# Gated cross-attention, experts, attention and FFN on one core: the middle stage's context, key weights and bias loaded and split inside the first attention's last units, and the opening's turns put first

## The chip, the cores and the metric

The kernel is one launch on one core of a Trainium2 chip. The metric is device time in microseconds, the median of three runs. All times below are microseconds unless they say ns.

## The reference

`x` is 2048 x 256, the context 1601 x 256, one batch. Four gated residual layers follow each other:

```python
x = x + tanh(g_xattn[0]) * L0_xattn(ctx, layernorm(x), mask, ...)  # 16 heads of 64; keys and values from the 1601 context rows and x
x = x + tanh(g_ffn[0]) * L0_ffn(layernorm(x), ...)                 # 8 experts, top 2, gelu
x = x + tanh(g_xattn[1]) * L1_xattn(layernorm(x), ctx, ...)        # 16 heads of 16, keys and values from the context
x = x + tanh(g_ffn[1]) * L1_ffn(layernorm(x), ...)                 # quantised, 1024 wide
```

The first attention runs over 3649 keys (2048 rows of `x` and 1601 of the context) for 2048 queries: in each layer softmax(q k^T) v, a product with the output weights, a gate, and the residual.

## The kernel before, in words

Four stages follow each other, each a block of five instruction streams that synchronise by semaphores, with a barrier between stages: `stage_latent` (L122, the first attention), `stage_middle` (L1544, the experts together with the key and value projections of the second attention), `stage_cross` (the second attention) and a quantised feed-forward stage. Every product that must be near fp32 is made of three fp16 passes: a value is split into a high part (ScalarE casts) and a low part (the difference, on GpSimd or VectorE).

**First attention.** The work is cut into 8 groups of two heads and 4 query blocks of 512, 32 units in all; a unit runs over 29 tiles of 128 keys. For a tile, TensorE makes the scores (`scores`, L914), ScalarE the exponential into a ring of six buffers `prob` (`weigh`, L480), TensorE the product with the values (`values`, L929). The row sums are built by adding the 29 `prob` tiles: VectorE adds five of them (`dve_tiles`, `add`, L630), GpSimd the other 24 (`pool_tiles`, L348), and `add_up` (L354) joins the two sums on GpSimd. A `prob` buffer is free again when its product and its addition are done. `sums` (L937) spreads the total over partitions by a product with ones, VectorE inverts it in four pieces (L636) and multiplies (L641), `outputs` (L948) applies the output weights in two halves, and `residual` (L649) adds each half to `x`. These steps of unit w are placed by tile numbers into unit w + 1; for unit 31 they stand at the end. Beside this, the running maximum of the unit after is made from pairs of score blocks (`pair`, L885 on TensorE, L598 on VectorE); the pairs run 33 ahead (`lead`), so they end in unit 30.

**Opening.** Before the first unit, `x` and the context are normalised on VectorE (L692 for `x`, L699 for the context), turned by TensorE (`turn_rows`, L826), scaled and cast on ScalarE (L501, L506), and the low part is made on GpSimd (`row_low`, L364). Three staging rows (`staged`) are used in turn, so the ScalarE row n waits until the low part of row n - 3 is made. The context rows are filled by VectorE (`fill_ctx`, L709), with masked values that GpSimd makes (L404). The 20 projections of group 0 (`open_jobs`; 8 key chunks, 4 query blocks, 8 value groups; L845, L853) use four PSUM banks in the order of `open_uses`: five stand before the first pair, the rest after every second pair (`job_after_pair`). In the main loop, the order on TensorE at the first tile is pair 33, then the scores of tile 0.

**Middle stage.** At its start, SyncE issues the loads of the context (1601 KB), the weights of the second attention (four groups of 384.5 KB through two staging buffers), the bias and the expert weights. ScalarE and GpSimd scale and split them (`w_high` L1708, `c_high` L1719, `e_high` L1727, `w_split` L1648, `c_split` L1655, `e_split` L1663). `x` is measured (L1825), normalised (L1838), turned (L1954) and split. TensorE projects keys of group 0, routes (`route`, L1965), projects the values of all groups, then the keys of groups 1 to 3 (`project`, L1987, L1994; ScalarE evacuates, L1742, L1738; VectorE makes the low key part, L1854). Finished key groups are laid into `k_op` by 12 small DMAs each; the keys of group 2 share a buffer with those of group 0, and of group 3 with group 1, so ScalarE's evacuation of group 2 waits until the 12 DMAs of group 0 have landed. The laying waits also for `ones_of` (L1668), which GpSimd does last of all. After that the 32 expert steps run (`first` L2010, `spread` L2020, `second_layer` L2036). The first `spread` waits for all projections and their low parts.

## Time and profile before

| | |
|---|---|
| median of three runs | 3250.26 (3250.1 to 3251.94) |
| the profiled execution: its own time | 3252.86 |
| its span, first to last instruction | 3251.1 |
| TensorE busy | 2952.4 (91%) |
| VectorE busy | 2419.8 (74%) |
| GpSimd busy | 2118.1 (65%) |
| ScalarE busy | 1806.9 (56%) |
| mean granted TensorE clock | 0.973 |
| DMA, mean over the span | 9 GB/s |

The span lies 1.8 below the execution's own time, which is launch and end around it. The page's 40 slices show TensorE at nine tenths or more everywhere but in the first slice and in the slices 29 and 30, where the first attention ends and the middle stage begins. The longest chain of waits on the page covers only the very end of the program, so the places of this change are read from the timeline and from busy times by stretch.

### The profile page before, as it was taken

The numbers are of one execution on the slowest core, as the hardware profiler recorded it, in microseconds if no ns is written. First come the engines' busy times: TensorE is split into PE (matmuls) and PEld (weight loads), VectorE is DVE, ScalarE is ACT, GpSimd is POOL, SyncE is SP. The second block draws the span as 40 slices with busy tenths as digits, with TensorE's granted clock in tenths as the row PEclk, the third lists the DMA queues.
The fourth block names the chain that finished last, engine by engine and source line by source line (L and its number), as shares of the span: only waits on it lengthen the run. The fifth ranks groups of instructions, "written<-read, shape, count | busy, mean of one in ns | idle before, by whom it ended". The sixth has DMA issues, their size and how long they took to land. (4 is left out here: it accounts for less than half of the span.)

```text
span 3251.1 us, 53579 instructions
## 1 busy us (share of the span) xinstructions
PE 2952.4 (91%) x21712; PEld 1091.0 (34%) x21720; DVE 2419.8 (74%) x2991; ACT 1806.9 (56%) x2025; POOL 2118.1 (65%) x1017
## 2 busy tenths in 40 slices
PE   5899999999999999999999999999498699999988
PEld 3233333333333333333333333322355123333235
DVE  8776787677777767777777876774435888888878
ACT  4455555455445555545555554545344388888875
POOL 5787988897898888889888888999520111111114
PEclk8999999999999999999999999999699699999999
DMA  1000000000000000000000000000210100000000
GB/s 62 6 1 1 1 8 1 1 7 1 1 7 1 1 1 7 1 1 7 1 1 1 3 1 1 1 1 1 68 33 9 46 7 7 8 7 7 7 1 27
DMA packets 24616, 28.73 MB, mean 9 GB/s; under 512 B 6511, under 2 KB 21296, under 8 KB 24370
## 3 DMA queue, kind: packets, MB, share of 16 engines
q1 hardware_dynamic: 24370, 25.31, 2.6%
q8 instruction: 172, 2.82, 0.4%
q14 instruction: 74, 0.61, 0.1%
HBM read 17.42 MB, written 2.10 MB: 6 GB/s over the span
## 5 line engine op out<-in xcount | busy, mean ns | idle before, releaser
L348 POOL TENSOR_TENSOR a_acc<-a_acc,a_prob 128x1024 f32<-128x1024 f32 x704 | 1725.3, 2451 | 299.5 <-ACT a_prob L480 217.7
L598 DVE TENSOR_REDUCE a_part_max<-wide 128x2 f32<-128x1024 f32 x880 | 1069.1, 1215 | 446.1 <-PE wide L885 445.3
L480 ACT ACTIVATE a_prob<-slot,a_mask_bias 128x1024 f32<-128x1024 f32 x928 | 986.9, 1112 | 740.7 <-PE slot L914 721.4
L929 PE MATMUL bank<-a_prob,a_val 128*64 128x512 f32 x3712 | 898.0, 606 | 2.1 <-ACT a_prob L480 2.1
L1218 ACT ACTIVATE a_prob<-slot,a_mask_bias 128x1024 f32<-128x1024 f32 x416 | 455.2, 1115 | 67.4 <-PE slot L1418 54.3
L885 PE MATMUL wide<-a_k_hi,a_q_hi 64*128 64x512 f16 (+1 forms) x2016 | 353.0, 362 | 113.8 <-DVE a_part_max L598 105.9
L1262 DVE TENSOR_REDUCE a_part_max<-wide 128x1 f32<-128x512 f32 x514 | 333.2, 682 | 37.7 <-PE wide L1406 21.0
L929 PEld LDWEIGHTS bank<-a_prob,a_val 128*64 128x64 f32 x3712 | 226.6, 136 | 394.2 <-issue 289.2
L914 PE MATMUL slot<-a_q_hi,a_k_lo 64*128 64x512 f16 x1856 | 352.7, 377 | 0.0
L914 PE MATMUL slot<-a_q_hi,a_k_step_hi 64*128 64x512 f16 x1728 | 328.2, 377 | 2.6 <-ACT a_prob L480 2.5
L914 PE MATMUL slot<-a_q_lo,a_k_step_hi 64*128 64x512 f16 x1728 | 328.0, 376 | 0.0
L885 PEld LDWEIGHTS wide<-a_k_hi,a_q_hi 64*128 64x128 f16 x2016 | 90.3, 93 | 551.4 <-DVE a_part_max L598 443.5
L1178 POOL TENSOR_TENSOR x_res<-a_gated,x_res 128x512 f32<-128x512 f32 x32 | 41.2, 1288 | 342.4 <-ACT a_gated L1230 342.2
L1432 PE MATMUL bank<-a_prob,a_val 128*32 128x256 f32 x3328 | 262.7, 392 | 0.1
L630 DVE TENSOR_TENSOR a_acc<-a_acc,a_prob 128x1024 f32<-128x1024 f32 x96 | 217.3, 2264 | 6.3 <-ACT a_prob L480 6.3
L1406 PE MATMUL wide<-a_k_op,a_q_op 48*128 48x512 f16 (+1 forms) x686 | 166.5, 355 | 36.6 <-DVE a_part_max L1262 29.0
L1262 DVE TENSOR_REDUCE a_part_max<-bank 128x1 f32<-128x512 f32 x254 | 173.3, 682 | 16.2 <-PE wide L1406 14.4
L1418 PE MATMUL slot<-a_q_op,a_k_op 64*128 64x512 f16 x832 | 160.9, 383 | 4.1 <-DMA a_q_op<-a_shift 2.8
L1166 POOL CAST a_hi<-a_y 128x512 f16<-128x512 f32 x15 | 9.2, 611 | 225.9 <-ACT a_y L1207 225.9
L636 DVE RECIPROCAL bank<-bank 128x128 f32<-128x128 f32 x128 | 120.7, 947 | 36.6 <-PE bank L937 36.6
L914 PEld LDWEIGHTS slot<-a_q_hi,a_k_lo 64*128 64x128 f16 x1856 | 90.5, 94 | 110.4 <-issue 0.8
L1406 PE MATMUL bank<-a_k_op,a_q_op 48*128 48x512 f16 (+1 forms) x338 | 109.6, 354 | 15.9 <-DVE a_part_max L1262 14.4
(398 smaller groups left out, 3275.0 us busy)
## 6 DMA issues: line engine op xcount, KB each, us to landing
a_w_staged<-in_w SPq DMA_DIRECT2D x8, 384.0 KB, 3.2
x_res<-in_x SPq DMA_DIRECT2D x4, 512.0 KB, 5.8
a_q_op<-a_hi SPq DMA_DIRECT2D x128, 16.0 KB, 1.8
out_x<-x_res SPq DMA_DIRECT2D x16, 128.0 KB, 1.7
a_k_op<-mid_k_hi SPq DMA_DIRECT2D x32, 52.0 KB, 2.2
mid_context<-in_ctxt SPq DMA_DIRECT2D x1, 1601.0 KB, 6.6
mid_w_staged<-in_w1a SPq DMA_DIRECT2D x4, 384.5 KB, 6.4
a_acc<-in_ctx SPq DMA_DIRECT2D x3, 512.0 KB, 8.4
```

Of the source, the lines that this page charges most:

```text
L348: nc.gpsimd.tensor_tensor(acc, before, prob[:, k % R, :], ALU.add).then_inc(added_p, 1)
L480: nc.scalar.activation(prob[:, k % R, :], m.slot[k % 2][:, :], ACT.Exp, bias=mbias[:, t:t + 1]).then_inc(probs_ready, 1)
L598: nc.vector.reduce_max(part_max[:, w % 2, :, j, c], pairs, AX.X).then_inc(max_used, 1)
L630: nc.vector.tensor_tensor(acc, before, prob[:, k % R, :], ALU.add).then_inc(added_v, 1)
L885: ins = nc.tensor.matmul(out, qh[g % 2][r, q0:q0 + P], src, start=True, stop=True, tile_position=(h * HALF, 0))
L914: ins = nc.tensor.matmul(score_bank(w, t, h), left, right, start=(whole and n == 0), stop=(n == len(terms) - 1), tile_position=(h * HALF, ...
L929: ins = nc.tensor.matmul(av[r, :], val[g % 2][:, t, r], prob[:, k % R, h * QB:(h + 1) * QB], start=(t == 0), stop=(t == NT - 1), tile_posi ...
L1218: nc.scalar.activation(prob[:, k % R, :], slot(("scores", w, s))[:, :], ACT.Exp, bias=mbias[:, t:t + 1]).then_inc(probs_ready, 1)
L1262: nc.vector.reduce_max(part_max[:, w % 2, 2 * z + h, j:j + 1, c], src, AX.X).then_inc(ring_used, 1)
L1406: ins = nc.tensor.matmul(bank(("max", n, h))[:, at:at + width_k], q_op[z][r, u * QB + j * P:u * QB + (j + 1) * P], k_op[g][z][r, k0:k0 + w ...
L1418: ins = nc.tensor.matmul(slot(("scores", w, s))[:, h * QB:(h + 1) * QB], k_op[g][z][r, t * P:(t + 1) * P], q_op[z][r, u * QB:(u + 1) * QB] ...
L1432: ins = nc.tensor.matmul(av[r, q], val[g][:, t, r], prob[:, (k + h // 2) % R, c0 + q.start:c0 + q.stop], start=(n == 0), stop=(n == a.halv ...
```

## The change

It does four things.

1. **Middle stage's inputs in the attention's last units.** A new function `keep_for_middle` lays one block of memory, `front_arena`, under the even buffers of the first attention (`k_hi`, `k_step_hi`, `q_hi`, `q_lo`, `val` of even groups). They are free after unit 27. From there the context, the weights of groups 0 and 1, the bias and the small expert arrays are loaded into them. GpSimd makes four memsets in unit 29; ScalarE scales and casts in unit 30 (`prepare`, 13 instructions behind odd tiles); VectorE makes the low parts and the bias in unit 31 (`prepare_low`). Three quarters of the statistics of `x` for the middle stage are taken in units 29 to 31 (`measure_final`). The second attention's `prob`, `y` and `bo` lie in the same block.
2. **Additions of the last unit.** In unit 31 VectorE adds nine tiles (`end_tiles`), GpSimd 20. `add_up` of unit 31 is gone: `sums` makes two accumulating products instead. The last inversion, multiplication and output product are done in halves, with a bank of their own for each half of the output.
3. **Middle stage.** It starts with key groups 0 and 1 (eight projections), two before each turn of `x`; then routing, the values of four groups, the keys of groups 2 and 3. `ones_of(0)` and `ones_of(1)` stand first on GpSimd.
4. **Opening.** Two projections stand before the first pair instead of five. GpSimd starts the low parts of `x` only after the normalisation of all `x`, and the masked values after the normalisation of the context. In unit 0, tile 0, the scores come ahead of pair 33.

```diff
+        self.job_after_pair = {1: keys_x[1], 3: keys_x[2], 5: keys_x[3], 7: keys_c[0], 9: v[0], 11: keys_c[1], 13: v[1], 14: queries[1],
+                               15: keys_c[2], 17: v[2], 18: v[3], 19: keys_c[3], 21: queries[2], 22: v[4], 23: v[5], 25: queries[3],
+                               27: v[6], 28: v[7]}
+        self.end_tiles = [3, 5, 7, 9, 13, 17, 21, 25, 27]
+        self.front_at = [(3, "scale", 0), (5, "keys", 0), (7, "queries", 0), (9, "scale", 1), (11, "keys", 1), (13, "queries", 1),
+                         (15, "router", 0)] + [(17 + 2 * c, "context", c) for c in range(4)]
+        self.low_at = [(1, "keys", 0), (2, "queries", 0), (3, "keys", 1), (4, "queries", 1), (5, "context", 0), (6, "context", 1),
+                       (7, "context", 2), (8, "context", 3), (13, "context", 4), (14, "context", 5), (15, "context", 6), (17, "context", 7),
+                       (19, "router", 0), (22, "bias", 0)]
...
+            sp.wait_ge(av_done, (last - NU + 1) * NT)
+            sp.dma_start(front.c32[:, :, 0:CTX], front.context.rearrange("(c p) t -> p c t", p=P)).then_inc(front_c, 16)
...
+            pool.wait_ge(normed, NL // 4)
+            row_low(0)
+            row_low(1)
             pool.wait_ge(w_first, 1)
             nc.gpsimd.tensor_tensor(w_lo[:, :], w_st[:, :], w_hi[:, :], ALU.subtract).then_inc(w_split, 1)
-            for n in range(6):
-                row_low(n)
+            row_low(2)
+            row_low(3)
+            pool.wait_ge(normed, len(cols))
             pool.wait_ge(mask_loaded, 32)
...
+            def divide_half(w, z):
+                dve.wait_ge(raw_ready, w + 1)
+                dve.wait_ge(inverted, a.pieces * w + a.pieces // 2 * (z + 1))
...
             def sums(w):
-                pe.wait_ge(total_ready, w + 1)
+                parts = [acc_p]
+                if w == last:
+                    pe.wait_ge(added_v, sum_v(w))
+                    pe.wait_ge(added_p, sum_p(w))
+                    parts = [acc_v, acc_p]
...
-        kinds = [("k", 0)] + [("v", g) for g in range(self.groups)] + [("k", g) for g in range(1, self.groups)]
+        kinds = [("k", 0), ("k", 1)] + [("v", g) for g in range(self.groups)] + [("k", 2), ("k", 3)]
...
-            turn(0, 0)
-            turn(0, 1)
-            project(0)
-            turn(0, 2)
-            project(1)
-            turn(0, 3)
-            project(2)
-            project(3)
+            for b in range(NB):
+                project(2 * b)
+                project(2 * b + 1)
+                turn(0, b)
             for b in range(NB):
                 route(b)
```

**Opening, GpSimd, before** (rows of the low parts, `xt_lo`, and of the masked values, `a_prob`; the names in brackets are the semaphores waited for):

```order
L398 TENSOR_TENSOR a_w_lo<-a_w_staged,a_w_hi 128x768 [waits a0_w_first,a0_wscale_set,a0_affine_loaded]
L362 COPY a_first_key<-a_k_full 128x1 [waits a0_rows_hi]
L363 TENSOR_TENSOR a_to_first<-a_affine_c,a_k_full 128x1
L364 TENSOR_TENSOR xt_lo<-a_k_full,xt_hi 128x512
L364 TENSOR_TENSOR xt_lo<-a_k_full,xt_hi 128x512 [waits a0_rows_hi] x4
L404 TENSOR_SCALAR a_prob<-a_valid_u,a_to_first,a_first_key 128x1664 [waits a0_affine_edge,a0_mask_loaded]
```

and of the change:

```order
L395 COPY a_first_key<-a_k_full 128x1 [waits a0_normed,a0_rows_hi,a0_wscale_set,a0_affine_loaded]
L396 TENSOR_TENSOR a_to_first<-a_affine_c,a_k_full 128x1
L397 TENSOR_TENSOR xt_lo<-a_k_full,xt_hi 128x512
L434 TENSOR_TENSOR a_w_lo<-a_w_staged,a_w_hi 128x768 [waits a0_w_first]
L397 TENSOR_TENSOR xt_lo<-a_k_full,xt_hi 128x512 [waits a0_rows_hi] x2
L441 TENSOR_SCALAR a_prob<-a_valid_u,a_to_first,a_first_key 128x1664 [waits a0_affine_edge,a0_mask_loaded,a0_normed]
```

Two low rows fewer stand before the masked values, and both places now wait for the normalised rows (`a0_normed`).

**Unit 31, VectorE, of the change** (`front_arena` holds the context and weights that came in; before, only four `a_acc` additions, four inversions, one multiplication and two residuals stood in this unit):

```order
L732 TENSOR_TENSOR front_arena<-front_arena 128x512
L735 TENSOR_TENSOR front_wq_lo<-front_arena,front_wq_hi 128x256
L751 TENSOR_TENSOR ct_lo<-front_arena,ct_hi 128x512 x2
L701 TENSOR_TENSOR a_acc<-a_prob 128x1024
L751 TENSOR_TENSOR ct_lo<-front_arena,ct_hi 128x512 x2
L701 TENSOR_TENSOR a_acc<-a_acc,a_prob 128x1024 x2
L707 RECIPROCAL bank<-bank 128x128 x2
L751 TENSOR_TENSOR ct_lo<-front_arena,ct_hi 128x512
L707 RECIPROCAL bank<-bank 128x128
```

In the whole unit twelve low parts of context and weights, the router's and three bias instructions are added, and VectorE has eight additions instead of four, beside GpSimd's 19 instead of 23.

**Start of the middle stage, TensorE, before** (`slot` from `ident` is a turn of `x`; `wide` and `bank` are key projections, `ct` the context):

```order
L1954 MATMUL slot<-ident,mid_xn 128x128 x16
L1987 MATMUL wide<-ct_hi,mid_kv_hi 128x512 x2
L1987 MATMUL wide<-ct_lo,mid_kv_hi 128x512 x2
L1987 MATMUL wide<-ct_hi,mid_kv_lo 128x512 x2
L1988 MATMUL wide<-mid_ones,mid_bias_op 128x512
L1954 MATMUL slot<-ident,mid_xn 128x128 x8
```

and of the change:

```order
L2093 MATMUL wide<-ct_hi,front_arena 128x512 x2
L2093 MATMUL wide<-ct_lo,front_arena 128x512 x2
L2094 MATMUL wide<-front_arena 128x512
L2063 MATMUL slot<-ident,mid_xn 128x128 x8
L2093 MATMUL bank<-ct_hi,front_arena 128x512 x2
L2093 MATMUL bank<-ct_lo,front_arena 128x512 x2
```

The projections lead; each turn of eight follows two of them.

## Rows read from the trace of the kernel before

**Rows 1.** Busy by stretch: time, five engines (PE, PEld, DVE, ACT, POOL), clock, DMA.

```profile
50.00:70.00 20.00, 16.12 (x145) 9.25 (x145) 19.59 (x21) 10.25 (x21) 14.75 (x16) 1.00 0.00 1
300.00:1000.00 700.00, 664.93 (x4392) 234.34 (x4392) 520.01 (x473) 364.19 (x410) 606.78 (x252) 1.00 0.01 3
2313.00:2336.00 23.00, 3.91 (x16) 3.14 (x16) 19.99 (x54) 9.26 (x18) 14.04 (x14) 0.50 0.65 221
```

**Rows 2.** Timeline of the opening, VectorE: start, length, what, idle before.

```profile
12.32 2.70 DVE L692 TENSOR_SCALAR a_prob<-x_res,a_mv,a_rstd 128x256 f32<-128x256 f32 x4
15.49 1.35 DVE L692 TENSOR_SCALAR a_prob<-x_res,a_mv,a_rstd 128x256 f32<-128x256 f32 x4
19.01 6.17 DVE L692 TENSOR_SCALAR a_prob<-x_res,a_mv,a_rstd 128x256 f32<-128x256 f32 x8
31.12 7.08 DVE L699 TENSOR_SCALAR a_acc<-a_acc,a_mv,a_rstd 128x256 f32<-128x256 f32 x13
46.10 0.75 DVE L709 SCALAR_TENSOR_TENSOR a_k_full<-slot,a_affine_c,a_prob 128x512 f32<-128x512 f32 x1 [7.30 <-PE slot L826]
49.69 1.22 DVE L598 TENSOR_REDUCE a_part_max<-wide 128x2 f32<-128x1024 f32 x1
91.26 1.22 DVE L598 TENSOR_REDUCE a_part_max<-wide 128x2 f32<-128x1024 f32 x1
```

**Rows 3.** Timeline of the opening, the other engines.

```profile
12.85 1.70 POOL L398 TENSOR_TENSOR a_w_lo<-a_w_staged,a_w_hi 128x768 f16<-128x768 f32 x1 [10.74 <-ACT a_w_staged L516]
28.57 1.15 POOL L364 TENSOR_TENSOR xt_lo<-a_k_full,xt_hi 128x512 f16<-128x512 f32 x1 [4.19 <-ACT xt_hi L506]
31.05 3.46 POOL L404 TENSOR_SCALAR a_prob<-a_valid_u,a_to_first,a_first_key 128x1664 f32<-128x1664 uint8 x2
92.62 0.61 PE L885 MATMUL wide<-a_k_hi,a_q_hi 64*128 64x512 f16 x2 [2.56 <-DVE a_part_max L598]
```

**Rows 4.** Unit 31's additions: group by line, and durations (ns min/median/max; VectorE's over all units).

```profile
L348 POOL TENSOR_TENSOR a_acc<-a_acc,a_prob 128x1024 f32<-128x1024 f32 x22 | 54.9, 2495 | 3.0
L348 POOL TENSOR_TENSOR a_acc<-a_acc,a_prob x22: 2337/2351/3155, 2240.1 to 2295.6; 128x1024 f32<-128x1024 f32 x22
L630 DVE TENSOR_TENSOR a_acc<-a_acc,a_prob x96: 1217/2172/3017, 121.4 to 2261.5; 128x1024 f32<-128x1024 f32 x96
```

**Rows 5.** Timeline of the attention's end.

```profile
2300.48 1.97 PE L937 MATMUL bank<-a_acc,a_ones 128*64 128x512 f32 x4 [15.07 <-POOL a_acc L354]
2302.50 3.40 DVE L636 RECIPROCAL bank<-bank 128x128 f32<-128x128 f32 x4 [36.59 <-PE bank L937]
2309.67 2.08 PE L948 MATMUL bank<-a_wo,a_att 128*128 128x256 f32 x4 [0.84 <-DVE x_res L649]
2311.79 0.75 DVE L649 SCALAR_TENSOR_TENSOR x_res<-bank,tanh_gates,x_res 128x512 f32<-128x512 f32 x1 [2.17 <-PE bank L948]
```

**Rows 6.** Middle stage, timeline; the DMA row is from its waits (total, times, longest).

```profile
2313.75 1.41 DVE L1825 BATCH_NORM_STATS2 mid_stats<-x_res 128x6 f32<-128x256 f32 x4
2317.35 2.48 DVE L1838 TENSOR_SCALAR mid_xn<-x_res,mid_mv,mid_rstd 128x256 f32<-128x256 f32 x4
2336.21 1.01 PE L1987 MATMUL wide<-ct_hi,mid_kv_hi 128*128 128x512 f16 x2 [5.99 <-DVE mid_bias_op L1869]
2340.69 1.29 DVE L1846 TENSOR_TENSOR xt_lo<-slot,xt_hi 128x512 f16<-128x512 f32 x2 [1.38 <-ACT xt_hi L1704]
2341.97 0.69 DVE L1854 SCALAR_TENSOR_TENSOR mid_k_lo<-wide,mid_k_hi 128x512 f16<-128x512 f32 x1
2347.18 0.29 DVE L1881 SCALAR_TENSOR_TENSOR mid_logits<-slot,moe_rb 128x128 f32<-128x128 f32 x1
2371.58 0.59 PE L2010 MATMUL slot<-xt_hi,mid_w_hi 128*128 128x512 f16 x2
ACT mid_k_hi L1742 <- DMA a_k_op<-mid_k_lo: 10.3, 2, 6.8
2394.58 0.58 PE L2020 MATMUL slot<-mid_wt_hi,mid_pick 128*128 128x512 f16 x1 [4.91 <-DVE mid_k_lo L1854]
```

More of the change, by code:

```diff
@@ L651, in measure, with measure_final @@
+            def measure_final(b):
+                dve.wait_ge(res_added, 2 * (last - NU + 1 + b) + 2)
+                for t in range(4 * b, 4 * b + 4):
+                    nc.vector.bn_stats(front.stats[:, t, :], m.x[:, t, :]).then_inc(front_measured, 1)
+                for t in range(4 * b, 4 * b + 4):
+                    dve.wait_ge(front_measured, t + 1)
+                    nc.vector.bn_aggr(front.mv[:, t, :], front.stats[:, t, :])
             def measure(src, t0, n):
@@ L980, in _ @@
                     n = w * NT + t + a.lead
+                    if w == 0 and t == 0:
+                        scores(w, t)
+                        pair(n)
+                        continue
                     if t % 2 == 0:
@@ L1003, in _ @@
                         project(*a.job_at[w * NT + t])
-            last = a.units - 1
             values(last, NT - 2)
@@ L1788, in _ @@
                 weights_high(g)
-                evacuate(NC + a.routing + g)
-            for p in range(NC + a.routing + NB, a.nj):
+                evacuate(a.front + a.routing + g)
+            for p in range(a.front + a.routing + NB, a.nj):
                 evacuate(p)
@@ L1906, in _ @@
                                         ALU.subtract).then_inc(wt_ready, 1)
-            for p in k_jobs[NC:]:
+            for p in k_jobs[a.front:]:
                 k_low(p)
@@ L2059, in _ @@
                 ins.then_inc(wt_turned, 1)
-                project(NC + a.routing + g)
+                project(a.front + a.routing + g)
             first(0)
             first(1)
-            for p in range(NC + a.routing + NB, a.nj):
+            for p in range(a.front + a.routing + NB, a.nj):
                 project(p)
```

499 lines of the change are left out of this document (281 added, 218 removed).

## The prediction

> **What bounds the kernel now.** I read the busy times by stretch first [rows 1]. In the attention's middle TensorE is busy 664.93 of 700 at clock 1.00: nothing is to be won there, and the change leaves it alone. At the start of the middle stage it is busy 3.91 of 23.00. Then the timelines of these places and of the opening, for who waits for whom.
>
> The opening: VectorE sits idle 7.30 before the first filled row, then makes 33 pairs nearly without a gap; the third starts at 49.69, the last at 91.26 [rows 2]. TensorE waits 2.56 for it, and only then makes pair 33 and the first scores [rows 3]. So VectorE sets the opening.
>
> Unit 31: GpSimd's 22 remaining additions take 54.9, with 3.0 of gaps, back to back: 2.495 each where the shortest takes 2.337 [rows 4]. TensorE gets the total at 2300.48, 15.07 late [rows 5]. GpSimd sets this unit.
>
> Middle stage: the first projection waits for the bias until 2336.21, routing is ready at 2347.18, the first expert matmul runs at 2371.58, the steps start at 2394.58, after ScalarE waited 10.3 for laying DMAs [rows 6].
>
> **Opening, part by part.** VectorE normalises four tiles in 1.35 alone and in 2.70 while a GpSimd operation of 1.70 runs beside it; eight take 6.17 beside the low rows [rows 2, 3]. GpSimd now keeps out: twelve tiles in 3 x 1.35 = 4.05 instead of 8.87, gain 4.8. The context's 13 tiles took 7.08; at 1.35 / 4 each they take 4.4, gain 2.7. They end at 38.2 - 7.5 = 30.7. One low part of a query (0.7), and the two first pairs run to 33.9, with the keys and queries that TensorE projected meanwhile. Here comes the new wait: GpSimd's masked values (3.46) start at 30.7 only, then low rows 4, 5 and 6 at 1.15 each [rows 3], 37.6, with row 7 of ScalarE and TensorE's turn of the context behind row 4. The fills (about 0.7 each) end at 38.7, where the third pair starts. It stood at 49.69: 11.0 earlier. From there VectorE's list is the old one, 91.26 + 1.22 - 49.69 = 42.8. Projections stand closer now (three behind consecutive pairs, twice), for which I charge 0.5. The first scores ahead of pair 33 fill part of TensorE's wait of 2.56 [rows 3]; between 0 and 2.56 I take 0.8. **Opening: -11.3.** Bounds: -6, if ScalarE's rows behind GpSimd cost 5 more; -14, if the removed gaps all count.
>
> **Units 28 to 31.** The loads go out on an idle SyncE queue, and the first who waits for them is GpSimd in unit 29, a whole unit later. ScalarE's 13 instructions in unit 30 stand behind odd tiles, where it waits for scores while TensorE makes the products: nothing. If this cover were gone, 13 x 0.69, the price of a 512-wide instruction [rows 6]: 9. The statistics (1.41 and 0.4 of aggregation [rows 6]) stand in VectorE's pair sequence in units 29 and 30, and TensorE's pairs wait for it: between nothing and 3.6 I take +1.0.
>
> In unit 31 GpSimd has 18 additions left instead of 22 and no joining. An undisturbed one is 2.337 plus its gap, 3.0 / 22 = 0.137: 2.474. VectorE's four additions and the rest lengthened them by 54.9 - 22 x 2.337 = 3.5, 0.87 for one. Now there are eight: 7.0. The low parts of context and weights, half as wide or less, I price at half: four before GpSimd reaches its second addition and six after, 2.1 + 1.9, the bias 0.5. GpSimd's 22 began at 2240.1; the 18 end at 2240.1 + 2.1 + 18 x 2.474 + 7.0 + 1.9 + 0.5 = 2296.1, against 2300.48: -4.4. `sums` doubles, +1.97 [rows 5]. The tail, 2302.50 to 2312.54 [rows 5], was four inversions (3.40), a multiplication, product, residual, product, residual: 10.0. In halves, with two banks: 3.40, two half multiplications at 0.4 (half a residual's 0.75), then one product (2.08) and one residual (0.75): 7.1, that is -2.9. **Unit 31 and tail: -5.3.** Bounds: 0, if every addition of GpSimd took nearly its longest, 3.155; -12, if VectorE disturbed nothing more than before.
>
> What the trace shows of the two engines is only that a VectorE addition of 1.217 at its shortest stretches to a median of 2.172, and GpSimd's to 3.155 [rows 4]. The Trainium skill, SBUF — State Buffer, "Who interferes with whom", says that a VectorE instruction with two SBUF inputs and a GpSimd one that reads SBUF exclude each other for a whole instruction. By it each new addition takes a full turn from GpSimd, and this is the second rival below.
>
> **Middle stage.** It starts as it did. Statistics of four tiles (1.41 and 0.4) instead of sixteen, the table load and square root to 2317.1, two normalisations beside GpSimd's memsets (2.48 and some 2.2 [rows 6]) and their waits: 2322.2. Then four blocks on VectorE: key low parts 6 x 0.6 + 2 x 0.25, turned low parts 4 x 1.25, two normalisations of 1.4 [rows 6] (a row's length overlaps the next by 0.1): 11.9, and 1.2 for waits on turns: 2335.3. TensorE's eight projections (two groups, 9.8), four turns (4) and a start at half clock (3) fit beside. With the last routing matmuls 2335.9, against 2347.0: -11.1. ScalarE then works down the same list as before, so the first expert matmul moves from 2371.58 to 2360.8. From there to the steps it was 23.0. A pair of 512-wide matmuls follows the next by some 0.43 (0.59 in the row of 2371.58 overlaps it), so a key chunk is 3 x 0.43 + 0.22 = 1.5 and a group, three chunks and a quarter, 4.9. Now two key groups remain instead of three, with 2.6 (six pairs) for the first expert matmuls and 1.2 for the last low part; the 10.3 for DMAs are gone, as group 0 and 1 are laid 25 earlier: 13.6, so -9.4. Sum -20.2; for the new rows' waits I take **-19.5**. Bounds: -13, if the waits between turns and low parts double and ScalarE's list starts 6 later; -22.
>
> **Sum.** -11.3 + 1.0 - 5.3 - 19.5 = -35.1. The profiled execution took 3252.86, 2.6 above the median; it would take 3217.8 with a span of 3216.0. On the median: 3250.26 - 35.1 = **3215.2**.
>
> **The rivals.**
> - *Opening held by GpSimd.* ScalarE's row 7, the turns and fills form a chain behind the masked values; if it costs 5 to 8 more, opening -3 to -6: about 3222. For it: three staging rows only. Against: it ends at 38.7, where before nothing of the pairs had begun.
> - *Strict turns on the shared memory path in unit 31.* Each of eight VectorE additions then takes 1.22 from GpSimd instead of 0.87, each low part 0.6 instead of 0.43: 2.8 + 1.8 = 4.6 more, 3219.8. For it: VectorE's median of 2.172. Against: four additions cost 3.5, not 4.9.
> - *All parts at their best bound*, GpSimd undisturbed: -14, -12, -22: 3203.
> - *The middle stage still waits*: its first projections cover little, because ScalarE's splitting list sets the first expert matmul. Then only the DMA wait and one key group go, -15: 3220.
> - *Slower: TensorE stays at 1.2 GHz.* Its work is now cut into short pieces between waits, in the opening from pair 2 on and in the middle stage's front. TensorE has 16.12 / 20 x 43 = 35 of work in the opening's last 43 [rows 1] and some 49 before the steps (eight groups of 4.9, 2.6, turns and routing 7). At half clock that is 70 and 98: the opening ends 16 after 92.5, the steps start 17 after 2394.58; with -5.3 and +1.0, 3279. It decides if the granted clock lies near 0.5 there. For it: clock 0.50 where TensorE had 3.91 of work in 23 [rows 1]. Against: 1.00 at 16.12 of 20 [rows 1], with the same pieces.
> - *The change has no effect*: a first projection that waits for its inputs again. The order has no such wait.
>
> **How the numbers follow.** Forecast 0.58, opening held 0.12, strict turns 0.09, all at best 0.08, middle waits 0.09, slower 0.03, no effect 0.01. A range from 3204 to 3229 takes in the forecast, three of the others whole and combinations of two of them. A measurement of this kernel can tell 0.2%, 6.5, from no change; only the clock rival lies above it. Faster 0.96, same 0.01, slower 0.03.
>
> **What would show it.** Third pair near 38.7; TensorE's pair 33 near 81.3, behind the first scores; a fill waiting for low rows near 37. In unit 31 (all 11 earlier) GpSimd's last addition 2.4 long some 56 after the joining of unit 30, then `sums` of 3.9. In the middle stage a projection at once, routing some 22 and steps some 61 after its start, no ScalarE wait for a DMA. I am wrong where the steps start over 67 after it, or where unit 31's additions average over 2.9.

## The result, and the profile after

| | before | changed |
|---|---|---|
| median of 4 runs, us | 3250.43 (3250.1 to 3251.94) | 3216.20 (3214.07 to 3217.43) |
| profiled execution, its span | 3251.1 | 3215.3 |

The ratio is 0.9893, 95% interval 0.9878 to 0.9909: 34.2 faster, where 35.1 were forecast. The profiled executions, cut at marks that both traces have (a unit's maxima complete, the shift of unit 31, the middle stage's first instruction, VectorE's first product of its steps):

| from ... to | before | changed | difference | forecast |
|---|---|---|---|---|
| start ... maxima of unit 1 | 151.38 | 139.69 | -11.7 | -11.3 |
| ... shift of unit 31 | 2070.44 | 2072.23 | +1.8 | +1.0 |
| ... start of the middle stage | 91.93 | 85.88 | -6.1 | -5.3 |
| ... VectorE's first product of the steps | 81.95 | 65.20 | -16.8 | -19.5 |
| ... end | 855.4 | 852.3 | -3.1 | 0 |

The pieces sum to 35.8, which is the difference of the two spans.

The timelines of the changed kernel (start, length, what, idle before). First the opening, VectorE's rows, which answer to [rows 2]:

```profile
12.28 1.38 DVE L802 TENSOR_SCALAR a_prob<-x_res,front_mv,a_rstd 128x256 f32<-128x256 f32 x4
...
17.04 2.67 DVE L802 TENSOR_SCALAR a_prob<-x_res,front_mv,a_rstd 128x256 f32<-128x256 f32 x8
26.65 4.29 DVE L809 TENSOR_SCALAR a_acc<-a_acc,front_mv,a_rstd 128x256 f32<-128x256 f32 x13
31.62 1.22 DVE L668 TENSOR_REDUCE a_part_max<-wide 128x2 f32<-128x1024 f32 x1
36.87 0.75 DVE L819 SCALAR_TENSOR_TENSOR a_k_full<-bank,a_affine_c,a_prob 128x512 f32<-128x512 f32 x1 [2.90 <-POOL xt_lo L397]
38.65 1.22 DVE L668 TENSOR_REDUCE a_part_max<-wide 128x2 f32<-128x1024 f32 x1
```

The forecast marks up to the third pair stand: normalisations of some 1.35 for four, their end near 31, a fill that waits for low rows at 36.87, the third pair at 38.65. TensorE makes the first scores before pair 33, which comes 1.8 later than forecast (81.3):

```profile
83.06 0.61 PE L1004 MATMUL wide<-front_arena 64*128 64x512 f16 x2 [0.28 <-DVE a_part_max L668]
```

This was 92.62 with a wait of 2.56 [rows 3]. Unit 31 and the attention's end, for [rows 4, 5], GpSimd, VectorE and TensorE:

```profile
2228.69 3.34 POOL L387 TENSOR_TENSOR a_acc<-a_acc 128x1024 f32<-128x1024 f32 x1
2231.99 23.47 POOL L381 TENSOR_TENSOR a_acc<-a_acc,a_prob 128x1024 f32<-128x1024 f32 x8
2255.89 29.65 POOL L381 TENSOR_TENSOR a_acc<-a_acc,a_prob 128x1024 f32<-128x1024 f32 x10 [0.43 <-POOL a_acc L381]
...
2229.73 5.61 DVE L751 TENSOR_TENSOR ct_lo<-front_arena,ct_hi 128x512 f16<-128x512 f32 x2
2264.61 2.73 DVE L743 CAST front_arena<-front_arena 2x1024 f16<-2x1024 f32 x1
2267.37 3.26 DVE L745 SCALAR_TENSOR_TENSOR front_arena<-front_arena,ident 2x1024 f16<-2x1024 f16 x1
...
2285.63 3.42 PE L1063 MATMUL bank<-a_acc,a_ones 128*64 128x512 f32 x8 [7.85 <-issue]
2289.10 1.78 DVE L707 RECIPROCAL bank<-bank 128x128 f32<-128x128 f32 x2 [10.72 <-PE bank L1063]
2295.78 0.75 DVE L726 SCALAR_TENSOR_TENSOR x_res<-slot,tanh_gates,x_res 128x512 f32<-128x512 f32 x1 [1.51 <-PE slot L1078]
```

GpSimd has 18 additions after the joining instead of 22, in 53.55. The tail, from the first inversion to the end of the last residual, takes 7.43 where it took 10.0. The middle stage, VectorE, for [rows 6]:

```profile
2297.80 1.40 DVE L1939 BATCH_NORM_STATS2 front_stats<-x_res 128x6 f32<-128x256 f32 x4
2301.49 7.35 DVE L1957 TENSOR_SCALAR mid_xn<-x_res,front_mv,mid_rstd 128x256 f32<-128x256 f32 x8
2311.16 1.36 DVE L1957 TENSOR_SCALAR mid_xn<-x_res,front_mv,mid_rstd 128x256 f32<-128x256 f32 x4
2323.09 0.29 DVE L1990 SCALAR_TENSOR_TENSOR mid_logits<-slot,front_rb 128x128 f32<-128x128 f32 x1 [0.93 <-PE slot L2072]
```

and GpSimd, TensorE and ScalarE there:

```profile
2297.73 5.90 POOL L1810 MEMSET a_k_op<- 128x1664 f16 x4 [12.20 <-POOLq L56]
2303.58 1.94 POOL L1814 MEMSET mid_wt_hi<- 128x2048 f16 x1
2305.47 1.94 POOL L1815 MEMSET mid_wt_lo<- 128x2048 f16 x1
...
2297.77 1.01 PE L2093 MATMUL wide<-ct_hi,front_arena 128*128 128x512 f16 x2 [2.03 <-PEq L56]
2307.61 1.97 PE L2063 MATMUL slot<-ident,mid_xn 128*128 128x128 f32 x8 [4.42 <-DVE mid_xn L1957]
...
2352.26 0.60 ACT L1869 ACTIVATE mid_k_hi<-wide 128x512 f16<-128x512 f32 x1 [3.69 <-PE wide L2094]
2360.99 1.28 ACT L1910 ACT_TABLE_LOAD   x1
```

TensorE projects at once, and no row of ScalarE waits for a DMA. But the eight normalisations take 7.35 instead of 4.7: the first four of them run beside GpSimd's memsets, each starts within one and ends about with it (0.72, 1.65, 1.97 and 1.96 long), and the other four, behind the last memset, have 0.4 each, as the next four have, 1.36 together. Routing is ready 25.3 after the start (forecast 22; before 33.4), the steps begin at 65.2 (forecast 61). The first expert matmul runs 50.16 after the start, before 57.83; from there to the steps it is 15.0 where it was 24.1.

### The profile page after: what moved, and what is told of

Read it like the earlier page. It is cut to its first block and busy times, and to the rows that moved or that the text cites. A ratio compares the mean times of both kernels' runs of the same rounds, so it can differ in the third digit from the quotient of the medians.

```text
span 3215.3 us, 53534 instructions
## 1 busy us (share of the span) xinstructions
PE 2952.3 (92%) x21716; PEld 1091.1 (34%) x21724; DVE 2459.1 (76%) x3006; ACT 1807.6 (56%) x2022; POOL 2099.6 (65%) x999
## 5 line engine op out<-in xcount | busy, mean ns | idle before, releaser
L527 ACT ACTIVATE a_prob<-slot,a_mask_bias 128x1024 f32<-128x1024 f32 x928 | 987.3, 1113 | 735.6 <-PE slot L1033 726.6
L1348 ACT ACTIVATE front_arena<-slot,a_mask_bias 128x1024 f32<-128x1024 f32 x416 | 455.3, 1116 | 63.0 <-PE slot L1548 49.6
L1048 PE MATMUL bank<-a_prob,a_val 128*64 128x512 f32 x1856 | 449.9, 607 | 0.2 <-ACT a_prob L527 0.2
L1048 PE MATMUL bank<-a_prob,front_arena 128*64 128x512 f32 x1856 | 447.6, 604 | 0.0
L1033 PE MATMUL slot<-front_arena 64*128 64x512 f16 x1856 | 276.7, 377 | 0.1
L1562 PE MATMUL bank<-front_arena,a_val 128*32 128x256 f32 x3328 | 261.5, 390 | 0.1
L1004 PE MATMUL wide<-a_k_hi,a_q_hi 64*128 64x512 f16 (+1 forms) x1024 | 179.4, 362 | 56.8 <-DVE a_part_max L668 53.1
L1004 PE MATMUL wide<-front_arena 64*128 64x512 f16 (+1 forms) x992 | 173.7, 363 | 57.1 <-DVE a_part_max L668 52.6
L1033 PE MATMUL slot<-a_q_hi,a_k_lo 64*128 64x512 f16 x928 | 176.8, 378 | 0.0
L1033 PE MATMUL slot<-front_arena,a_k_lo 64*128 64x512 f16 x928 | 176.3, 377 | 0.0
```

Of the source, the lines that this page charges most:

```text
L527: nc.scalar.activation(prob[:, k % R, :], m.slot[k % 2][:, :], ACT.Exp, bias=mbias[:, t:t + 1]).then_inc(probs_ready, 1)
L1004: ins = nc.tensor.matmul(out, qh[g % 2][r, q0:q0 + P], src, start=True, stop=True, tile_position=(h * HALF, 0))
L1033: ins = nc.tensor.matmul(score_bank(w, t, h), left, right, start=(whole and n == 0), stop=(n == len(terms) - 1), tile_position=(h * HALF, ...
L1048: ins = nc.tensor.matmul(av[r, :], val[g % 2][:, t, r], prob[:, k % R, h * QB:(h + 1) * QB], start=(t == 0), stop=(t == NT - 1), tile_posi ...
L1348: nc.scalar.activation(prob[:, k % R, :], slot(("scores", w, s))[:, :], ACT.Exp, bias=mbias[:, t:t + 1]).then_inc(probs_ready, 1)
L1562: ins = nc.tensor.matmul(av[r, q], val[g][:, t, r], prob[:, (k + h // 2) % R, c0 + q.start:c0 + q.stop], start=(n == 0), stop=(n == a.halv ...
```

## The experiments

All are edits of the changed kernel. The table has each one's time, the time of the kernel before beside it, and marks from its trace ("inversion": first inversion after the attention, from the shift of unit 31; "logits" and "table", ScalarE's table load ahead of the steps: from the middle stage's start). Each kernel has one trace.

| kernel | time / before | unit 1's maxima | inversion | logits | table |
|---|---|---|---|---|---|
| before | | 151.38 | 80.68 | 33.43 | 79.73 |
| changed | 3216.20 / 3250.43 | 139.69 | 77.18 | 25.29 | 63.19 |
| u31_five | 3223.03 / 3251.19 | 138.84 | 83.62 | 25.30 | 63.21 |
| u31_thirteen | 3215.36 / 3251.19 | 139.88 | 75.70 | 24.25 | 62.16 |
| u31_no_context_low | 3214.90 / 3251.19 | 138.63 | 75.35 | 24.44 | 62.34 |
| u31_bias_last | 3212.91 / 3251.70 | 141.73 | 72.69 | 25.49 | 63.38 |
| open_no_waits | 3217.31 / 3251.14 | 142.25 | 76.80 | 25.24 | 63.14 |
| open_old_order | 3227.17 / 3251.70 | 151.75 | 77.24 | 25.32 | 63.22 |
| open_pair_first | 3216.94 / 3253.42 | 141.87 | 77.33 | 25.46 | 63.36 |
| mid_memsets_behind | 3217.24 / 3251.19 | 139.13 | 77.35 | 25.30 | 64.83 |
| mid_memsets_last | 3212.16 / 3251.14 | 138.81 | 76.71 | 18.95 | 56.86 |
| mid_list_first | 3209.03 / 3251.14 | 139.72 | 76.65 | 19.33 | 55.99 |
| mid_one_key_group | 3223.19 / 3251.14 | 139.16 | 76.95 | 25.44 | 69.95 |
| all_together | 3205.90 / 3251.70 | 138.76 | 73.04 | 19.33 | 55.76 |

Where an edit leaves its piece alone, the inversion lies within 76.65 to 77.35 (8 kernels), the logits within 24.25 to 25.49, unit 1's maxima within 138.6 to 139.9 but for u31_bias_last, where the granted clock was lower there (told under open_pair_first). Whole runs differ by more than that for reasons told at the end, so the marks carry the verdicts.

### Unit 31: what does an addition on VectorE cost?

**u31_five.**

```diff
-        self.end_tiles = [3, 5, 7, 9, 13, 17, 21, 25, 27]
+        self.end_tiles = [5, 7, 9, 15, 17]
```

> The changed kernel with unit 31's additions divided as in every other unit: VectorE makes 4 of them instead of 8, GpSimd 22 instead of 18 after the joining of unit 30. In the changed kernel those 18 took 53.5 from 2231.99, 9.0 over 18 x 2.474. Theory A (the prediction's price: a VectorE addition costs GpSimd 0.87): GpSimd ends 4 x (2.474 - 0.87) = 6.4 later, time 3216.2 + 6.4 = 3222.6. Theory B (strict turns, 1.22 each): +5.0, 3221.2. Theory C (the 9.0 come from VectorE's low parts, its additions cost nothing): +9.9, 3226.1. GpSimd's mean addition in unit 31: 2.9 by A and B, 2.88 by C.

GpSimd's 22 additions, by line, from the joining on (total and mean in ns, then the gaps before them):

```profile
L381 POOL TENSOR_TENSOR a_acc<-a_acc,a_prob 128x1024 f32<-128x1024 f32 x22 | 57.2, 2599 | 3.3 <-POOL a_acc L381 0.4
```

The inversion comes 6.44 later (6.3 to 7.0 against the eight), so an addition moved is worth 1.61, and it costs GpSimd 2.474 - 1.61 = 0.86 (0.73 to 0.91): theory A. Strict turns (5.0) and free additions (9.9) fall. (The means in the expectation were worked out wrongly; by A it is (53.5 + 6.4) / 22 = 2.72, and the trace gives 2.60 with 0.15 of gap, 2.75.)

**u31_thirteen**: `end_tiles` with every odd tile from 3 to 27, thirteen of them, so VectorE makes twelve additions.

> The other direction: 13 tiles of unit 31 on VectorE, that is 12 additions, GpSimd has 14 after the joining of unit 30. A: GpSimd's last addition ends 6.4 earlier, 3209.8. B: 5.0 earlier, 3211.2. C: 9.9 earlier, of which 6.6 can count, since TensorE's last product of values ends at 2277.8 only, 7.8 before the sums. Theory D: VectorE, which has low parts, statistics and four quarters of inversion besides, is the later of the two now, its late additions keep ring places and ScalarE's exponentials wait for them: sums no earlier, 3216 to 3221.

Only 1.5 come. GpSimd's rows show why:

```profile
2232.38 24.26 POOL L381 TENSOR_TENSOR a_acc<-a_acc,a_prob 128x1024 f32<-128x1024 f32 x8
2262.14 2.36 POOL L381 TENSOR_TENSOR a_acc<-a_acc,a_prob 128x1024 f32<-128x1024 f32 x1 [5.50 <-ACT a_prob L527]
2266.88 2.36 POOL L381 TENSOR_TENSOR a_acc<-a_acc,a_prob 128x1024 f32<-128x1024 f32 x1 [2.37 <-ACT a_prob L527]
```

It is idle 9.85 for exponentials (five waits). VectorE's additions are late behind its low parts and the bias, the ring's places stay taken, and ScalarE waits. That is D's mechanism; the time it forecast (no gain) was a little too high. The next experiment moves the bias to try it.

**u31_bias_last**: thirteen tiles, and

```diff
-                       (19, "router", 0), (22, "bias", 0)]
+                       (19, "router", 0)]
...
                     add(last, t - 2)
+            prepare_low("bias", 0)
             for z in range(2):
```

> As the kernel with 13 tiles of unit 31 on VectorE, and its three instructions on the bias (6.7 beside GpSimd's additions) stand behind VectorE's last addition, where it waits for the sums. With 13 tiles alone the first inversion came 75.70 after the shift of unit 31 (77.18 in the changed kernel, 83.62 with 5 tiles), and GpSimd waited 9.9 for exponentials, which waited for ring places held by VectorE's late additions. Theory A (VectorE's work ahead of its last additions sets the sums now): without 2 to 6.7 of it the inversion comes 72 to 74 after the shift, time 3211 to 3213. Theory B (the total of both engines' turns on the memory is full either way): 75 to 76, 3215.

72.69: theory A. VectorE's bias work now lies in its wait for the sums, and the inversion comes 3.0 earlier than with thirteen tiles and 4.5 earlier than in the changed kernel.

**u31_no_context_low**: the eight `"context"` entries of `low_at` are gone, so this kernel leaves out the low parts of the context.

> Left out: the eight low parts of the transposed context in unit 31, so the middle stage's products with them use what an earlier block left there; all other work stays. It measures what they cost. The prediction priced each at 0.43 of GpSimd's time, six of them behind its second addition: -3 to -3.5, 3213. By strict turns 0.6 each: -4 to -5, 3211.5. If a low part holds GpSimd for as long as it shows in the trace beyond its 0.6 (2.8 for a 512-wide one): -8 or more, down to TensorE's values at 2277.8 (-6.6), 3209.5. If they are free: 3216.

The 18 additions take 52.59 instead of 53.55 and begin 1.13 closer to the shift; the inversion comes 1.83 earlier (1.3 to 2.0 against the eight kernels). So the eight cost some 2, not 8 x 0.43 = 3.4. Their length in the trace is not their price: two 512-wide ones show 5.61 in the changed kernel, and all eight cost 2.

### The opening: waits or order?

**open_no_waits**

```diff
-            pool.wait_ge(normed, NL // 4)
             row_low(0)
...
-            pool.wait_ge(normed, len(cols))
```

> The opening without GpSimd's two waits for the normalisations: its low rows, the weights' low part and the masked values may run beside them again. Theory A (the prediction's: what runs beside a normalisation of four tiles takes 1.35 more): the twelve tiles take 8.9 instead of 5.4, the context's 7.1 instead of 4.3; TensorE's pairs begin 6 later, the third stands at 43 to 45 instead of 38.65, the first exponential at 87 to 89 instead of 82.88: 3221. Theory B (the chain of GpSimd behind its waits, masked values and low rows, sets the third pair): it runs earlier now, the third pair stands at 38 or before, 3213 to 3216.

VectorE in its opening:

```profile
18.12 9.19 DVE L800 TENSOR_SCALAR a_prob<-x_res,front_mv,a_rstd 128x256 f32<-128x256 f32 x8
32.70 5.12 DVE L807 TENSOR_SCALAR a_acc<-a_acc,front_mv,a_rstd 128x256 f32<-128x256 f32 x13
38.34 1.21 DVE L666 TENSOR_REDUCE a_part_max<-wide 128x2 f32<-128x1024 f32 x1
42.36 1.22 DVE L666 TENSOR_REDUCE a_part_max<-wide 128x2 f32<-128x1024 f32 x1
```

The contention is there (9.19 for 2.67), the first pair is 6.7 later, the third only 3.7 and the maxima of unit 1 only 2.6: masked values and low rows, done early here, no longer hold a fill (VectorE waits 0.35 before the first one, not 2.90). A has the mechanism, B the reason why half of it doesn't count.

**open_old_order**: the opening's tables and program order of before, with the two waits kept.

```diff
-        open_uses = [("rows", n) for n in range(6)] + [("proj", 0, a.open_jobs[0])] + [("rows", 6), ("rows", 7)]
-        open_uses.append(("proj", 0, a.open_jobs[1]))
+        open_uses = [("rows", n) for n in range(4)] + [("proj", 0, i) for i in a.open_jobs[0:2]]
+        open_uses += [("rows", 4), ("rows", 5), ("proj", 0, a.open_jobs[2]), ("rows", 6), ("rows", 7)]
+        open_uses += [("proj", 0, i) for i in a.open_jobs[3:5]]
...
-                if n % 4 == 2 and n // 4 < len(ctx_loaded):
+                if n % 4 == 0 and n // 4 < len(ctx_loaded):
```

> The changed kernel with the opening's order of before on TensorE, ScalarE and VectorE (context turns and fills ahead of pairs 0, 4, 8 and 12, five projections ahead of the first pair, the rest one behind every other pair), but with GpSimd's two waits for the normalisations and the first scores ahead of pair 33, as changed. Maxima of unit 1 are complete at 139.69 in the changed kernel, at 142.25 without the waits, at 151.38 before. Theory A (the prediction's working: 7.5 of the gain is the undisturbed normalisations, which these waits give): 144 to 146, time 3221 to 3223. Theory B (without the waits only 2.6 were lost, so the order is worth the other 9): the normalisations end near 31, but the first fill waits for the masked values and low rows ahead of every pair, maxima at 148 to 151, 3226 to 3228.

VectorE and GpSimd:

```profile
32.35 0.24 DVE L857 RECIPROCAL a_rstd<-a_std 128x13 f32<-128x13 f32 x1 [6.78 <-ACT a_std L551]
32.83 4.29 DVE L815 TENSOR_SCALAR a_acc<-a_acc,front_mv,a_rstd 128x256 f32<-128x256 f32 x13
48.67 0.75 DVE L825 SCALAR_TENSOR_TENSOR a_k_full<-slot,a_affine_c,a_prob 128x512 f32<-128x512 f32 x1 [10.96 <-PE slot L951]
...
37.23 3.44 POOL L440 TENSOR_SCALAR a_prob<-a_valid_u,a_to_first,a_first_key 128x1664 f32<-128x1664 uint8 x2 [10.59 <-DVE a_acc L815]
```

Theory B: 151.75, as late as before (151.38). The normalisations are short, and nothing comes of it. ScalarE takes the context's deviation behind two projections and two rows (a wait of 6.78), GpSimd's masked values start at 37.23, and VectorE stands 10.96 before the first fill. The time saved on the normalisations turned into these waits: before, VectorE waited 0.29 for that deviation and 7.30 for the first fill. Unit 0's maxima come even 2.6 later than before (89.71 against 87.14), and unit 0 itself, 2.2 shorter than before, gives that back.

**open_pair_first**: the case `if w == 0 and t == 0` of TensorE's loop is taken out.

> The changed kernel without its special case for the first tile of unit 0: TensorE makes pair 33 ahead of the first scores again. Theory A (the prediction's 0.8, from between 0 and the 2.56 that TensorE waited there before): the maxima of unit 1, complete at 139.69 in the changed kernel, come at 140.5, time 3217. Theory B (unit 0 took 64.24 from maxima to maxima before and 62.01 in the changed kernel, and the whole 2.2 is this): 141.9, 3218.4. Theory C (what ScalarE starts earlier waits later, and unit 0's length comes from elsewhere): 139.7, 3216.

141.87, 2.2 later, is theory B's number; the first exponential moves from 82.88 to 85.71. From unit 0's maxima to unit 1's it is 64.05, as 64.24 before, where eleven of the kernels with the first scores ahead have 61.8 to 62.5. But the twelfth, u31_bias_last, has 63.82 with the order of the changed kernel, and there TensorE's granted clock was low. The same 12 in open_pair_first and in u31_bias_last:

```profile
80.00:92.00 12.00, 7.95 (x44) 2.94 (x46) 7.81 (x8) 4.28 (x4) 5.25 (x4) 0.72 0.09 33
80.00:92.00 12.00, 9.87 (x44) 2.82 (x46) 8.03 (x8) 4.46 (x4) 5.97 (x4) 0.57 0.11 33
```

The changed kernel had 0.86 there, the kernel before 0.72 (89.5 to 101.5). So with the same order and a lower clock unit 0 takes 1.8 longer, and how much of the 2.2 is the order and how much the clock isn't separated: no kernel with the first scores ahead has 0.72. Whether the order is worth theory A's 0.8 or theory B's 2.2 stays open. The time of the traced run does not show the 2.2, because units 29 and 30 together took 2.8 less in this trace, see the last section.

### The middle stage: what holds routing, what holds the steps?

**mid_memsets_behind** and **mid_memsets_last**: a wait ahead of GpSimd's memsets. In the first it is

```diff
+            pool.wait_ge(normed, 8)
             ones_of(0)
```

and in the second `NX`, sixteen, instead of 8.

> The middle stage's first memsets on GpSimd (9.8 from the stage's start) wait until VectorE has normalised eight tiles. In the changed kernel these eight took 7.35 beside them, where the later ones, with GpSimd idle, took 1.36 for four. Theory A (the memsets slow VectorE down, and VectorE's list bounds routing): the eight take 2.8, the logits come 4.5 earlier, 20.8 after the stage's start instead of 25.3, and ScalarE's list and the steps follow: 3211.7. Theory B (TensorE at half clock bounds the front: its projections of key groups 0 and 1 and turns): the eight take 2.8, the logits come only 1 to 2 earlier, 3214.5 to 3215.5. Theory C (the eight are slow for another reason): nothing changes.

> GpSimd's first memsets of the middle stage wait for all sixteen normalisations of VectorE. With them behind eight, the eight took 2.68 instead of 7.35, but the next four 5.84 instead of 1.36, and the logits stood at 25.3 after the stage's start as before. Theory A (the memsets' 9.8 cost the normalisations 4.6 wherever they overlap, and VectorE's list bounds routing): all sixteen take 5.4, the logits come at 20.7, ScalarE's list follows, its table load for the steps (63.2 after the stage's start in the changed kernel) at 58.6, time 3211.7. Theory B (ScalarE's splitting or TensorE at half clock bounds what follows): the logits come earlier, the steps by less than 2.

Normalisations in the first, then in the second:

```profile
2298.76 2.68 DVE L1958 TENSOR_SCALAR mid_xn<-x_res,front_mv,mid_rstd 128x256 f32<-128x256 f32 x8
2303.73 5.84 DVE L1958 TENSOR_SCALAR mid_xn<-x_res,front_mv,mid_rstd 128x256 f32<-128x256 f32 x4
```

```profile
2297.33 2.68 DVE L1958 TENSOR_SCALAR mid_xn<-x_res,front_mv,mid_rstd 128x256 f32<-128x256 f32 x8
2302.31 1.39 DVE L1958 TENSOR_SCALAR mid_xn<-x_res,front_mv,mid_rstd 128x256 f32<-128x256 f32 x4
```

Behind eight, the collision only moves, from 7.35 + 1.36 to 2.68 + 5.84, the logits stay at 25.3, and the table comes 1.6 later. None of the three theories had that reason. Behind sixteen it is gone: logits at 18.95, table at 56.86, both 6.3 earlier, time 3212.16. Of the 6.3, 4.6 are the normalisations, and 1.4 are waits of VectorE that are gone, those for TensorE's key projections by way of ScalarE above all (total 5.46 in the changed kernel, 4.10 here); the last 0.3 was not traced. Two stretches of the stage, the changed kernel and then this one:

```profile
2297.80:2305.00 7.20, 5.39 (x14) 1.75 (x14) 5.44 (x13) 2.67 (x4) 7.20 (x5) 0.69 0.87 266
2305.00:2313.00 8.00, 5.39 (x24) 3.41 (x25) 7.52 (x14) 1.59 (x3) 2.41 (x2) 0.57 0.47 122
```

```profile
2293.64:2300.80 7.16, 7.16 (x28) 3.17 (x29) 5.41 (x20) 3.65 (x6) 0.00 (x0) 0.69 0.87 279
2300.80:2308.80 8.00, 7.82 (x54) 4.80 (x52) 8.00 (x19) 4.31 (x9) 1.76 (x2) 1.00 0.43 112
```

In the changed kernel TensorE idles 4.42 before its first turn and is granted 0.57 in the second stretch, where its turn of 1.05 takes 1.97; without the gap it has 1.00. Two kernels with the same middle stage as the changed one, u31_thirteen and u31_no_context_low, were granted 0.79 where it had 0.58 (8.0 to 16.0 after the stage's start), and their logits come at 24.25 and 24.44 instead of 25.29: the clock is worth about 1 here.

**mid_list_first**: the memsets last, and

```diff
                 x_high(0, b)
+                if b == 1:
+                    w_high(2)
+                if b == 2:
+                    w_high(3)
...
-            w_high(2)
...
-            w_high(3)
```

> As the kernel with the memsets last, and ScalarE splits the weights of groups 2 and 3 (2.05 each) between the rows of the front, where it idles (4.94 before the first rows, 2.39 later), not in the list behind the logits, which it works through without a gap from 2326.77 to 2348.57. Theory A (ScalarE's list sets the first expert matmul and with it the last two key groups): the steps come 4.1 earlier still, the table load for them 54.5 after the stage's start, time 3207.6. Theory B (the splits delay rows and key groups in the front, or GpSimd's subtractions bound): 1 or less of it is left, 3211. Slower than with the memsets last alone, if the weights land late and ScalarE waits for them.

Theory B by the number: of 4.1 only 0.9 comes. ScalarE's list is 4 shorter, but it now waits for TensorE's value projections. GpSimd's low parts of the experts' weights end at 2336.90, just before the first expert matmul, but TensorE doesn't stand for them: from 2332.79 to the end of the projections its rows follow each other without a gap, and its one longer wait ahead of that is 1.40, for ScalarE.

```profile
2327.93 8.97 POOL L1805 TENSOR_TENSOR mid_w_lo<-moe_w,mid_w_hi 128x512 f16<-128x512 f32 x8 [3.73 <-ACT mid_w_hi L1857]
2337.43 0.59 PE L2119 MATMUL slot<-xt_hi,mid_w_hi 128*128 128x512 f16 x2
```

**mid_one_key_group**: `kinds` as before the change; VectorE's low key parts follow the new order.

```diff
-        kinds = [("k", 0), ("k", 1)] + [("v", g) for g in range(self.groups)] + [("k", 2), ("k", 3)]
+        kinds = [("k", 0)] + [("v", g) for g in range(self.groups)] + [("k", 1), ("k", 2), ("k", 3)]
```

> The middle stage projects key group 0 and value group 0 in its front and key group 1 only behind the values, as before the change; all else is as changed. The prediction gave the shorter end behind the first expert matmul 9.4: one key group (4.9) and the wait of ScalarE for laying DMAs. Theory A: the table load for the steps comes 9 later, at 72 after the stage's start, with a wait of ScalarE for a DMA of some 4, the logits up to 2.6 earlier: 3225. Theory B (group 0 is laid long before, so no wait returns): only the key group, less what VectorE saves in the front, 66 to 68: 3219 to 3221.

```profile
2330.77 0.27 PE L2101 MATMUL wide<-front_arena,ct_hi 128*128 128x128 f16 x2 [4.49 <-POOL front_wq_lo L1797]
...
2364.04 1.09 ACT L1869 ACTIVATE mid_k_hi<-wide 128x512 f16<-128x512 f32 x2 [4.81 <-DMA a_k_op<-mid_k_lo]
```

The table comes 6.8 later, between A and B. The DMA wait of 4.81 is back as A said, and the logits don't come earlier: in the front the key group was free. The 6.8 are not a clean price of the 9.4, though, since value group 2 now comes up so early that TensorE waits 4.49 for the low part of its weights.

**all_together**: memsets last; groups 2 and 3, the experts' bias and first weights split in the front; `first(0)`, `first(1)` behind key group 2; thirteen tiles and the late bias in unit 31.

```diff
-            first(0)
-            first(1)
             for p in range(a.front + a.routing + NB, a.nj):
                 project(p)
+                if p == a.front + a.routing + NB + NC - 1:
+                    first(0)
+                    first(1)
```

> The version that should beat both: memsets of the middle stage behind its normalisations; ScalarE splits the weights of groups 2 and 3 and the experts' bias and first weights in the front, the second weights behind four values; TensorE projects key group 2 ahead of the first expert matmuls, which waited for the experts' low parts; 13 tiles and the late bias in unit 31. With memsets and weights alone the table load for the steps came 55.99 after the stage's start. Theory A (ScalarE's list and TensorE's wait for the experts' low parts set it): 51 to 53; with unit 31's 2 to 4, 3203 to 3206. Theory B (TensorE's projections of values and keys, 32 of them in all, bound it already): 55 to 56, 3206 to 3209. Worse if the experts' weights are not loaded when ScalarE wants them.

3205.90 against 3251.70, ratio 0.9860 (0.9845 to 0.9874): 11.6 more off the kernel before than the change alone (45.8 against 34.2). The middle stage follows B, 55.76: from the stage's first projection to its last TensorE has one wait, of 0.23. The time lies in A's range all the same; unit 31 gave 4.1 (73.04).

## Why the prediction was right, step by step

- **Opening, -11.3, measured -11.7.** The sum held, and the third pair stood where it was put. The reason given for it held by half: the working gives 7.5 to undisturbed normalisations. Taking the waits out of the new order costs 2.6 (142.25), putting them into the old order gains nothing (151.75 with the first scores moved, 151.38 before). Shorter normalisations are worth something only where the order has the work behind them ready. Behind the third pair two terms were too small, in opposite directions, and that they cancelled is luck. The lead of 11.0 was 9.5 at pair 32 (81.80 against 91.26): 1.6 lost where 0.5 was charged to the projections' closer stand. The charge itself held, since open_no_waits, with the same stand, loses 0.6 between the same pairs; the other 1.0 is gone without GpSimd's waits, and 0.88 of it stands in the changed kernel as a wait of VectorE for a pair behind the second fill (41.88). And unit 0 gave 2.2, not 0.8; how much of that are the first scores and how much a better granted clock (0.86 against 0.72) is not separated.
- **Units 28 to 31, +1.0, measured +1.8 from unit 1 on.** Of it 1.1 lie in units 29 and 30 (130.7 and 131.8, with a granted clock of 0.97 in both units of both traces), 0.7 in the units before. The size held. Which of the statistics, the memsets and the casts costs the 1.1 was not tried.
- **Unit 31 and tail, -5.3, measured -6.1.** The 18 additions: 53.9 by the sum, 53.55 in the trace. The price of 0.87 for an addition was measured as 0.86. `sums` 3.42 instead of 3.9, the tail 7.43 instead of 7.1. The context's low parts cost 2 where the price of 0.43 makes 3.4; that the 53.55 fit all the same means that the bias, the router or the weights' low parts cost more, and these were not tried apart. (The terms 2.1 and 1.9 don't follow from that price either: four and six at 0.43 are 1.7 and 2.6.) The rival of strict turns falls by its number. The Trainium skill, SBUF — State Buffer, "Who interferes with whom", calls the shared port pair an exclusive lock. VectorE's rows agree with that (a 256-wide low part of 2.59 beside GpSimd additions of at least 2.34), GpSimd's loss of 0.86 for a VectorE addition of 1.22 does not.
- **Middle stage, -19.5, measured -16.8.** Direction and mechanism held, the DMA wait is gone. (The sum has a slip: -11.1 and -9.4 are -20.5, not -20.2.) The term that was mis-sized is "two normalisations beside GpSimd's memsets (2.48 and some 2.2)" in routing's -11.1: they took 7.35, and behind the gap that they left TensorE its granted clock was 0.57 for 8. Routing gained 8.1. The 2.2 was an estimate where the trace of before has a row, the second four beside GpSimd's work:

```profile
2323.59 3.94 DVE L1838 TENSOR_SCALAR mid_xn<-x_res,mid_mv,mid_rstd 128x256 f32<-128x256 f32 x4
```

From the logits to the steps -8.6 were measured and -8.4 forecast. The rival in which the middle stage still waits falls: routing and the first expert matmul (-7.7) did move. So does the one in which TensorE stays at 1.2 GHz: it was granted 0.94 from the third pair to pair 32, 0.78 up to the logits and 1.00 from there to the steps.
- **After the steps, 0 forecast, -3.1 measured.** No instruction was changed there, only the place of three buffers. Up to the cross attention's table load it is -0.6, in the cross attention -4.2, and in the last stage +1.7. The last two go in large part with the granted clock, see the last point below. That this nearly gave back what the middle stage fell short of is luck, and the total of 34.2 against 35.1 is closer than the working was.

## What to carry to other kernels

When an operation is lengthened by a neighbour engine, moving the neighbour is worth something only if it moves clear of all such operations (memsets behind eight normalisations: nothing; behind sixteen: 6.3), and only if the chain behind is ready to use the time (the opening's waits without its order: nothing). Price a shared path by the change in the bounding engine's total, not by how long the other engine's rows look. Before two traces are compared, compare the granted clock of the same stretch in both. And before handing more work to an idle engine, look at what stands ahead of it in that engine's program: a late addition there keeps a ring place, and the wait shows up two engines further on.

## What was not expected of the hardware

- A memset of 1.49 to 1.94 on GpSimd, which reads nothing, makes a VectorE normalisation that takes 0.41 alone wait for nearly its whole length: four took 5.84 where four alone take 1.39, one for each memset. Statistics (1.40 for four) and operations that read PSUM (1.29 for two) had their usual length beside the same memsets. The section of the Trainium skill named above says that `tensor_scalar` in a two-port mode takes the shared pair, and that a VectorE instruction with at most one SBUF input outside such a mode does not contend. That the normalisation contends and the statistics don't fits, but no row shows its mode: it starts every 0.32, as slowly as statistics of the same width (0.33).
- The same attention takes several lengths, with TensorE's granted clock. From the maxima of unit 29 to those of unit 31, that is units 29 and 30, it took 128.8 to 129.1 in open_no_waits, open_pair_first, mid_list_first and both memset kernels, where the clock was 1.00 in both units; 130.4 to 130.7 in the three kernels with 0.97 in one of them; and 131.6 to 131.9 in the five with 0.97 in both, the changed one among them (the kernel before, with a different program there: 0.97 in both, 130.7). All but the kernel before have the same program in these units. Unit 30 of the changed kernel and of mid_memsets_last:

```profile
2143.75:2209.24 65.49, 60.88 (x375) 19.43 (x373) 51.46 (x50) 38.14 (x45) 58.80 (x25) 0.97 0.00 1
2141.63:2205.54 63.91, 59.37 (x375) 19.23 (x373) 51.07 (x50) 38.14 (x45) 58.71 (x25) 1.00 0.00 1
```

  So 2.8 of a run's time hang on it. Why the clock falls in one run of the same instructions and not in another stays open.
- The granted clock in the first 11.53 of the cross attention's exponentials takes three values. Ahead of it ScalarE waits 48 to 49 in all kernels, and TensorE, which works in short pieces there, is granted 0.50 to 0.57. The stretch before the change and after it:

```profile
2568.47:2580.00 11.53, 9.49 (x40) 1.82 (x38) 7.37 (x12) 8.26 (x8) 5.67 (x8) 0.50 0.03 8
```

```profile
2535.22:2546.75 11.53, 9.03 (x58) 2.22 (x58) 8.23 (x14) 9.21 (x9) 5.67 (x8) 0.74 0.03 8
```

  In six traces it is 0.73 or 0.74, and from the cross attention's table load to that of the last stage they take 578.7 to 578.9; in six 0.65, 580.1 to 581.4; in two 0.50, all_together with 581.5 and the kernel before with 582.9. all_together has the changed kernel's program there, so 2.8 of the 4.2 by which the changed kernel's cross attention is shorter than before go with the clock; the other 1.4 stays open. The last stage then takes 100.9 to 104.7; the shortest had the highest mean clock in it (0.92), the longest the lowest (0.83). Its last stretch before the change and after it, with the same numbers of instructions:

```profile
3230.10:3250.10 20.00, 13.31 (x93) 8.92 (x92) 14.87 (x28) 8.23 (x9) 0.00 (x0) 1.00 0.10 34
3192.60:3212.60 20.00, 15.09 (x93) 10.02 (x92) 14.82 (x28) 8.25 (x9) 0.00 (x0) 0.86 0.08 27
```

  Ahead of it both have 0.89. The three traces with 0.89 and then 1.00 (the kernel before, open_old_order, mid_one_key_group) take 100.9 to 101.0 for the last stage, the changed one 102.7. The edits lie hundreds of microseconds away from both places. In its profile the change had the good clock in the cross attention and the bad one at the end.
